# Cross-attention with float32r splits: the output projection in three passes, the heads' chunks split in place, and some low parts moved from GpSimd to VectorE

## The reference, cut to what matters

```python
qh, kh, vh = heads(xn @ Wq), heads(ctx @ Wk), heads(ctx @ Wv)   # 8 heads of 128; 2048 rows each
sim  = qh @ kh.T                                # per head 2048 x 2048
attn = softmax(1.5 * sim * 128 ** -0.5)         # over the keys (the mean shift falls out)
out  = concat(attn @ vh) @ Wout + bout          # Wout: 1024 x 256
x    = x + out
```

## Time and profile before

| | |
|---|---|
| median of 3 runs | 1329.42 us |
| profiled execution, its own time | 1332.3 us |
| span from its first to its last instruction | 1330.2 us |
| busy: PE, DVE, ACT, POOL | 1287.7, 1023.5, 895.9, 907.9 us |
| mean granted clock of TensorE | 0.99 |

### The profile page before, as it was taken

One profiled execution on the slowest core, in us unless ns is written; L12 is line 12 of the kernel. 1 busy time (PEld: TensorE's weight loads), 2 busy tenths in 40 slices (PEclk: granted clock), 3 DMA queues, 4 the chain that ended last, 5 costly groups with the idle time before them and its releaser, 6 DMA issues. The chain is left out here.

```text
span 1330.2 us, 22729 instructions
## 1 busy us (share of the span) xinstructions
PE 1287.7 (97%) x8358; PEld 1077.1 (81%) x8358; DVE 1023.5 (77%) x1628; ACT 895.9 (67%) x1315; POOL 907.9 (68%) x645
## 2 busy tenths in 40 slices
PE   5999999999999999999999999999999999988998
PEld 4688888888887788888888888888888888777998
DVE  6355498759317889999999999999999899985554
ACT  4555433425655878878778778778787777775774
POOL 2544410225410899989989999999999989863553
PEclk9999999999999999999999999999999999997999
DMA  6703032246764989988888888888888888796672
GB/s 219 104 6 74 4 101 81 67 130 245 208 233 140 247 213 231 221 196 216 215 203 215 216 201 218 215 196 221 214 201 217 201 191 208 185 252 244 203 230 76
DMA packets 172377, 241.35 MB, mean 181 GB/s; under 512 B 34179, under 2 KB 78085, under 8 KB 172272
## 3 DMA queue, kind: packets, MB, share of 16 engines
q1 hardware_dynamic: 155040, 208.11, 62.0%
q10 hardware_dynamic: 15184, 25.96, 5.7%
q0 software_dynamic: 2048, 5.90, 1.1%
HBM read 64.79 MB, written 41.32 MB: 80 GB/s over the span
## 5 line engine op out<-in xcount | busy, mean ns | idle before, releaser
L1217 POOL TENSOR_TENSOR xa_pT<-xa_moved,xa_pT 128x1024 fp32r<-128x1024 f32 x246 | 589.0, 2428 | 27.1 <-ACT xa_pT L1735 26.0
L1557 PE MATMUL xa_S<-xa_kT,xa_qT 128*128 128x512 f32 x1536 | 389.1, 401 | 1.2 <-ACT xa_probs L1741 1.2
L1741 ACT ACTIVATE xa_probs<-xa_S,xa_mx_nb_rinv 128x1024 f32<-128x1024 f32 x256 | 285.9, 1117 | 146.8 <-DVE xa_mx_nb_rinv L1339 146.8
L1574 PE MATMUL xa_O<-xa_pT,xa_v 128*128 128x512 f32 x1536 | 377.2, 394 | 2.9 <-DVE xa_pT L1392 2.6
L1336 DVE TENSOR_REDUCE xa_mx_nb_rinv<-xa_S 128x1 f32<-128x1024 f32 x256 | 305.3, 1211 | 78.1 <-PE xa_S L1557 78.0
L1574 PEld LDWEIGHTS xa_O<-xa_pT,xa_v 128*128 128x128 f32 x1536 | 289.0, 189 | 69.9 <-DVE xa_pT L1392 2.9
L1557 PEld LDWEIGHTS xa_S<-xa_kT,xa_qT 128*128 128x128 f32 x1536 | 288.5, 188 | 67.9 <-ACT xa_probs L1741 2.9
L1349 DVE STREAM_TRANSPOSE xa_tq<-xa_probs 128x1024 f32<-128x1024 f32 x256 | 316.7, 1238 | 15.0 <-ACT xa_probs L1741 7.3
L1735 ACT ACTIVATE xa_pT<-xa_moved 128x1024 fp32r<-128x1024 f32 x254 | 253.9, 1050 | 2.1 <-PE xa_O L1574 1.1
L506 PE MATMUL fw_pp<-fw_hT,fw_wqk 128*128 128x512 f32 x384 | 95.0, 405 | 4.3 <-DVE fw_hT L647 4.3
L506 PEld LDWEIGHTS fw_pp<-fw_hT,fw_wqk 128*128 128x128 f32 x384 | 73.4, 194 | 20.7 <-DVE fw_hT L647 3.0
(11 more groups left out here) (247 smaller groups left out, 1679.1 us busy)
## 6 DMA issues: line engine op xcount, KB each, us to landing
xa_moved<-xa_tq SPq DMA_DIRECT2D x508, 256.0 KB, 4.5
heads_k<-ci_outs SPq DMA_DIRECT2D x32, 256.0 KB, 2.0
heads_v<-ci_outs SPq DMA_DIRECT2D x32, 256.0 KB, 2.3
heads_q<-ci_outs SPq DMA_DIRECT2D x32, 256.0 KB, 2.4
xa_chunk<-heads_v ACTq DMA_DIRECT2D x32, 256.0 KB, 4.2
ex_w1s<-in_L_ffn_w_dram SPq DMA_DIRECT2D x8, 1024.0 KB, 7.3
ex_w2s<-in_L_ffn_w_dram SPq DMA_DIRECT2D x8, 1024.0 KB, 9.7
xa_chunk<-heads_q ACTq DMA_DIRECT2D x31, 256.0 KB, 4.2
```

Source lines behind the costliest of these rows:

```text
L1217: pool.tensor_tensor(quadrants(pT[LO], r), unit_moved(r), quadrants(pT[HI], r).bitcast(F32), ALU.subtract).then_inc(lo_ready, 1)
L1557: last = pe.matmul(banks[:, k % 2], qT[a][:, i // GT % 2, q], kT[b][h % 2][:, k * 512:(k + 1) * 512], start=(n == 0), stop=(n == 2))
L1574: last = pe.matmul(O[:], v[a][:, j * P:(j + 1) * P], pT[b][:, r % PRING, k], start=(j == 0 and n == 0), stop=(j == JT - 1 and n == 2))
L1741: act.activation(probs[:, unit % RING], S[:, score_banks(unit)].rearrange("p a b -> p (a b)"), ACT.Exp, bias=nb[:, s % 2:s % 2 + 1], scale ...
```

## The change

1. **Output projection in three passes for groups 0 to 27** (heads 0 to 6, `SPLIT_GROUPS` = 28). ScalarE's `split_high(g)` writes the high part of `oT` (512 columns), and once per head that of `woh` (256 columns). VectorE's `split_low(g)` subtracts for the low parts, that of oT written over oT itself. `out_project` then issues 6 float32r matmuls of 256 columns per half in place of 2 float32 ones, and its first half waits for VectorE's low part. Its slots and those of `add_output` are one later.
2. **Chunks are split in place.** The ring of two is gone. A chunk is loaded into the region of its own low part (`raw_k`, `raw_v`, `raw_q`), and the subtraction writes over it. Its load is issued at the end of the slot before the one in which it is split, and waits for the region's last reader first. The chunks are spread differently over a head's slots.
3. **Low parts of q's chunks on VectorE.** `q_low` is run by VectorE in the slot after ScalarE's high part; only head 0's first q chunk stays with GpSimd.
4. Small ones: head 0's v chunks wait on ScalarE, not GpSimd, for the stores that share their space; the load of `woh` waits for the split of the last one and not for the last projection; the constants of the routing wait for the last split group's projection.

```diff
-        CRING, RING, MRING, PRING = 2, 2, 3, 4
+        RING, MRING, PRING = 2, 3, 4
...
+        raw_k = [home(f"xa_rawk{i}", f"kT{i}", [P, TOK], F32, LO * 4 * TOK) for i in range(2)]
+        raw_v = home("xa_rawv", "v", [P, TOK], F32, LO * 4 * TOK)
+        raw_q = home("xa_rawq", "qT", [P, 2, GCOLS], F32, LO * 4 * 2 * GCOLS)
         woh = sb("xa_wout", [P, D])
-        chunk = home("xa_chunk", "chunk", [P, CRING, UNIT])
+        wohs = [home(f"xa_wouts{a}", "chunk", [P, D], F32R, 4 * (GCOLS + D * a)) for a in (HI, LO)]
...
+        SPLIT_GROUPS = SLOTS // GT - 4
...
-            return SLOTS + OUTPUTS[g, k] if (g, k) in OUTPUTS else (g + 1) * GT + LAG + 2 * k
+            return SLOTS + OUTPUTS[g, k] if (g, k) in OUTPUTS else (g + 1) * GT + LAG + 2 * k + (g < SPLIT_GROUPS)
...
-            plan = {0: ("k", h + 1, 0), 1: ("q", h, 1), 2: ("k", h + 1, 1), 3: ("k", h + 1, 2), 4: ("v", h, 0),
-                    5: ("q", h, 2), 6: ("v", h, 1), 7: ("v", h, 2), 8: ("v", h, 3), 9: ("k", h + 1, 3),
-                    10: ("q", h, 3), 13: ("q", h + 1, 0)}
+            plan = {0: ("k", h + 1, 0), 1: ("q", h, 1), 3: ("k", h + 1, 1), 4: ("q", h, 2), 5: ("v", h, 0), 6: ("v", h, 1),
+                    7: ("v", h, 2), 8: ("v", h, 3), 10: ("q", h, 3), 11: ("k", h + 1, 2), 13: ("q", h + 1, 0),
+                    14: ("k", h + 1, 3)}
...
+        def q_split_at(s):
+
+            return [c for c in chunks_of(s - 1) if c[0] == "q"] if s > 0 else []
+
+        def group_split_at(s):
+
+            g, phase = divmod(s - LAG - GT, GT)
+            return g if phase == 1 and 0 <= g < SPLIT_GROUPS else None
...
@@ vector
+            def q_low(c):
+                dve.wait_ge(chunk_hi, place[c] + 1)
+                dve.tensor_tensor(target(c, LO), staged(place[c]), target(c, HI).bitcast(F32),
+                                  ALU.subtract).then_inc(out_lo, 1)
+
+            def split_low(g):
+                if g % 4 == 0:
+                    dve.wait_ge(out_hi, g + g // 4 + 1)
+                    dve.tensor_tensor(wohs[LO][:], woh[:], wohs[HI][:].bitcast(F32), ALU.subtract).then_inc(out_lo, 1)
+                dve.wait_ge(out_hi, g + g // 4 + 2)
+                dve.tensor_tensor(oTs[LO][:], oT[:], oTs[HI][:].bitcast(F32), ALU.subtract).then_inc(out_lo, 1)
...
                     maxima(s)
+                if s < SLOTS:
+                    for c in q_split_at(s):
+                        q_low(c)
+                    if group_split_at(s) is not None:
+                        split_low(group_split_at(s))
                 if 1 <= s <= SLOTS:
                     transpose(s - 1, 1)
...
@@ tensor, out_project
+                if k == 0 and g < SPLIT_GROUPS:
+                    pe.wait_ge(out_lo, outputs_split(g))
...
+                    if g < SPLIT_GROUPS:
+                        for n, (a, b) in enumerate(PARTS):
+                            last = pe.matmul(output_bank(g, k)[:, m], oTs[a][:, t], wohs[b][:], start=(n == 0), stop=(n == 2))
...
@@ scalar
+            def split_high(g):
+                if g % 4 == 0:
+                    act.wait_ge(wo_in, 16 * (g // 4 + 1))
+                    act.wait_ge(y_mm, 2 * g)
+                    act.activation(wohs[HI][:], woh[:], ACT.Copy).then_inc(out_hi, 1)
+                act.wait_ge(oT_ready, g + 1)
+                act.activation(oTs[HI][:], oT[:], ACT.Copy).then_inc(out_hi, 1)
...
+                if GT <= p and p % GT == 0 and p // GT - 1 < SPLIT_GROUPS:
+                    split_high(p // GT - 1)
                 if s < SLOTS:
                     for c in chunks_of(s):
                         chunk_high(c)
+                    for c in chunks_of(s + 1) if s + 1 < SLOTS else ():
+                        load(place[c])
```

More of the change, by code:

```diff
@@ L904, in cross_block @@
         first_in = [sem(f"xa_first_in{i}") for i in range(FIRST)]
-        chunk_in = [sem(f"xa_chunk_in{i}") for i in range(CRING)]
+        chunk_in = sem("xa_chunk_in")
         chunk_hi, chunk_lo = sem("xa_chunk_hi"), sem("xa_chunk_lo")
@@ L1063, in staged @@
                 return moved[:].rearrange("p r q j n -> p (r q j n)")[:, n * UNIT:(n + 1) * UNIT]
-            return chunk[:, n % CRING]
+            kind, h, part = order[n]
+            cols = slice(part * UNIT, (part + 1) * UNIT)
+            if kind == "k":
+                return raw_k[h % 2][:, cols]
+            return raw_v[:, cols] if kind == "v" else raw_q[:, part % 2]
         def target(c, a):
@@ L1205, in chunk_low @@
                 n = place[c]
[L1206 to L1210, removed]
                 pool.wait_ge(chunk_hi, n + 1)
@@ L1701, in load @@
             def load(n):
[L1702 to L1705, removed]
-                act.dma_start(chunk[:, n % CRING], source(order[n])).then_inc(chunk_in[n % CRING], 16)
-            def chunk_high(c):
-                n = place[c]
-                kind, h, part = c
-                if n < FIRST:
-                    act.wait_ge(first_in[n], 16)
-                else:
-                    act.wait_ge(chunk_in[n % CRING], 16 * ((n - FIRST) // CRING + 1))
+                c = kind, h, part = order[n]
                 if kind == "k" and h >= 2:
@@ L1718, in chunk_high @@
                     act.wait_ge(sim_done, 2 * GT * (4 * h + part - 1))
-                if kind == "v" and h == 0 and part == QUADS - 1:
+                if kind == "v" and h == 0:
                     for u in range(UNITS - OUTS, UNITS):
-                        if u % OUTS == 0:
+                        if u % OUTS == part + 1 or part == QUADS - 1 and u % OUTS == 0:
                             written(act, u)
@@ L1724, in chunk_high @@
                     act.wait_ge(pv_done, 2 * (TILES * h - GT + part) + 2)
+                for u in units_of(c):
+                    written(act, u)
+                act.dma_start(staged(n), source(c)).then_inc(chunk_in, 16)
+            def chunk_high(c):
+                n = place[c]
+                if n < FIRST:
+                    act.wait_ge(first_in[n], 16)
+                else:
+                    act.wait_ge(chunk_in, 16 * (n - FIRST + 1))
                 act.activation(target(c, HI), staged(n), ACT.Copy).then_inc(chunk_hi, 1)
-                if FIRST + CRING <= n + 1 < len(order):
-                    load(n + 1)
             def high_part(r):
@@ L1785, in _ @@
                 copy_out(n)
-            for n in range(FIRST, FIRST + CRING):
-                load(n)
             act.wait_ge(w_lo, 2)
```

52 lines of the change are left out of this document (36 added, 16 removed).

## The result

The kernel after takes 1412.33 us (median of 4 runs, 1408.99 to 1413.80) against 1330.19 us before: a ratio of 1.0614 (95% interval 1.0591 to 1.0636), 82 us slower. The forecast was 1398 us, within 1355 to 1425. Its profiled execution has a span of 1410.5 us against 1330.2, 80.3 us more, and the clock that TensorE was granted is 0.98 in the mean.

The account below looks back on a forecast made before the run. TensorE bound the kernel before; waits for GpSimd would make VectorE the bound, at 105.3 us per head against 95.5. Seven heads at +9.8 give 69 us, so a median of 1398 us, range 1355 to 1425.

Parts of the forecast that it names:

- The bound now, and the slack: Attention slots before the change: TensorE sets the pace at 95.5 us per head; VectorE works 89.3, leaving 6.2 slack.
- The wait as cause: VectorE's new two-SBUF-input instructions wait until GpSimd's running instruction ends, 0.97 us, making VectorE the bound.
- Its size: VectorE's added work per head: seven single instructions at 1.45 us, 10.1, plus the woh and oT pair, 4.1; sum 14.2.
- 0.45 x 4 = 1.8 per head: VectorE's wait for scores queued behind the first projection half, which waits for the low part: 1.8 us per head.
- The sum over VectorE's whole load: VectorE's 89.3 + 14.2 = 103.5 us per head against TensorE's 94.6; with score waits 105.3, +9.8 per head.
- only the last could count, 1.5 us: Head 0's first three q low parts, slots 2, 5 and 11: only slot 11's could cost, 1.5 us.
- Three passes, 0.11 us per half: Projection on TensorE: six float32r matmuls take 0.71 us, each half 0.11 us cheaper, 0.9 us per head.
- Chunks in place at nothing: Chunk loads, issued about one slot (6 us) ahead, land after 4.0 us, 5.5 at most; cost nothing.
- What was to show: Signs: new VectorE instructions 1.2 to 2.0 us, VectorE close to 100%, TensorE about 90%, ScalarE waiting longer for nb, slots 6.6.
- No waiting (1335 and 1323): Rivals without GpSimd waits: late low part stalls TensorE, 1335 us, chance 0.07; or TensorE stays the bound, 1323, chance 0.05.
- Much slower: Rival: VectorE meets each GpSimd instruction at its start, wait 2.41 us, +21.3 per head, 1478 us; chance 0.06 up to that.

Follow-up runs that it names:

- run 2: Kernel after, with VectorE's new low parts written by a one-element reduce_max (copies, subtraction left out): 1332.47 us, ratio 1.0014.
- run 7: Kernel after, with oT's low part subtracted from PSUM a slot earlier, q's and woh's on GpSimd, projection at its old slots: 1330.66 us.
- run 5: Kernel after, plus 20 float32 matmuls of 128 columns on TensorE before the projection's wait in every fourth group: 1401.42 us.
- q_gpsimd: Kernel after, with q's low parts back on GpSimd and the projection split kept: 1408.13 us; four executions took 1386.4 to 1413.9.
- swap: Kernel after, with oT's and woh's low parts moved to GpSimd and q's left on VectorE: 1365.61 us; executions 1358.0 to 1374.1.
- run 6: Kernel after, with q's low parts on GpSimd and oT's and woh's written by one-element maxima, subtraction left out: 1327.02 us.
- run 3: Parts of the change alone; for chunks in place, kernel after with plain float32 projection and q's low parts on GpSimd: 1330.85 us.
- run 9: Kernel after, with GpSimd's low parts of the probabilities in four 512-column instructions per slot instead of two of 1024: 1422.45 us.

## Why the prediction was right, and where it was off

- **The bound now, and the slack.** Right. In the five heads between slots 28 and 108 VectorE was busy 87.2 us per head before and waited 6.4 for the scores (6.2 in the prediction).
- **The wait as cause.** Right. In run 2 the price goes away with the wait, at the same number of instructions in the same places; in run 7 the real subtraction stands on VectorE without waiting, though a slot earlier and without q and `woh` beside it.
- **Its size.** Near, and in part by luck. VectorE's busy time grew from 435.89 to 506.13 us over those five heads, 14.05 per head, where the sum said 14.2:

```profile
584.10:1116.76 532.66, 490.45 (x2161) 393.76 (x2160) 506.13 (x605) 393.51 (x585) 447.10 (x201) 0.98 0.77 189
```

  The single ones take 1.61 us in the mean by their records, which is 1.54 without the overlap of 0.07, instead of 1.45: a wait of 1.06 instead of 0.97 (11.24 us for seven, less 0.55 each). The pair takes 4.5 instead of 4.1 from start to start. That makes 15.2 for the nine, 1.0 more than the sum, and VectorE's other instructions came out 1.2 shorter beside them, partly by more overlap of their records.
- **Waiting for the scores after a projection, "0.45 x 4 = 1.8 per head".** This is the term that was mis-sized. VectorE waits 3.9 us per head for them (19.3 us in 50 waits over the five heads), of which 2.02 + 1.14 stand behind `woh` and oT alone. The prediction worked with scores at full clock, but behind the stall of 4.68 us the clock is down. With the clock held, run 5, the waits are 10.0 us in 50, or 2.0 per head, near the predicted value. So per head 14.05 - 6.4 + 3.9 = 11.55, less 0.7 by which VectorE's other gaps shrank, is the 10.85 measured; 9.8 was predicted. Over seven heads the difference grows by 75.5 us (slots 12 to 124) instead of 69.

```profile
DVE xa_mx_nb_rinv L1373 <- PE xa_S L1613: 19.3, 50, 2.0
```

- **The sum over VectorE's whole load.** The forecast lets every wait count in full once VectorE's slack is spent, wherever it stands. That fits the whole change and fails for its parts, so the near hit on the total is luck to that extent. In the forecast's terms the split of the projection without q is 3 x 1.45 + 4.1 = 8.5 on VectorE, which with the slack of 6.2 and 1.8 for the scores makes +4 us per head; `q_gpsimd` shows 7.86, and VectorE there still waits 5.9 us per head for the scores (29.5 us over the five heads), nearly the 6.4 of before. q alone on VectorE would be 5.8, inside the slack, so next to nothing; `swap` shows 4.98 in the trace of its slowest execution (about 0.8 of it behind oT), and even its fastest is 28 us above before. What the runs show in its place is a price by slot: where the projection waits for the low part (5.2 to 6.7 us with `woh`, 0.65 to 1.8 without) TensorE and VectorE stop in turn, and room in other slots doesn't make up for it, while the four q of the kernel after cost about 2 us per head net by their steps.
- **Head 0, "only the last could count, 1.5 us".** Off: 4.5 us at slot 12, by the q that lost to two GpSimd instructions, and 5.5 in all up to there. 75.5 + 5.5 = 81.0, and the spans differ by 80.3.
- **Three passes, 0.11 us per half.** Right: six matmuls from 709.65 to 710.36 are 0.71 us, plain slots gain 0.05 to 0.12, and run 6 keeps 0.71 us per head of 0.9. **Chunks in place at nothing**: right by run 3. **ScalarE's copies at nothing**: right by runs 2 and 6, which have them and lose nothing.

```profile
709.65 0.40 PE L1650 MATMUL xa_Y<-xa_wouts,xa_oT_hi 128*128 128x256 f32 x2
...
710.36 0.87 PE L1613 MATMUL xa_S<-xa_kT,xa_qT 128*128 128x512 f32 x3
```

- **What was to show.** The instructions at 1.2 to 2.0 us in the mean: q is (1.32), oT is a little above (2.15), those after `woh` are 2.82 (2.9). VectorE close to 100%: it is 95.0 over the five heads. TensorE about 90%: 92% (490.45 of 532.66). ScalarE's idle time per exponential did grow, but more than half of it is now for the transposes (67.9 us from 600 to 1100 us) and not for nb (60.3 us). Slots of 6.6 us: 6.66.
- **The rivals.** No waiting (1335 and 1323): refuted, and runs 2 and 6 (1332.5 and 1327.0 us) show that these times were fair for that case. Much slower, a whole instruction waited each time: not here in the mean, but the q at 466.81 and run 9 show that single ones can wait as long and longer.

## What to carry to other kernels

Before low parts or other work on two SBUF inputs move to VectorE, look at what GpSimd does in that slot: the price isn't only the instruction's 0.6 us but the rest of the GpSimd instruction that is running, too, and a free share of VectorE's time doesn't pay for it where TensorE waits behind it in the same slot. An operand left in PSUM took the wait away here, 653 ns against 2149, at the price of holding the bank. And a stall of TensorE is to be counted with the lower clock after it, which here made 5.2 to 6.7 us out of 3.92.

## What the runs showed that I had not expected

- `tensor_scalar` with one SBUF input waits for GpSimd (1760 and 1066 ns in the mean), a maximum over one element with the same input and output doesn't (676 ns).
- GpSimd waits for VectorE too: 2.85 us instead of 2.40 for the instruction that stands behind one of VectorE's.
- A waiting instruction can lose to more than one GpSimd instruction: two of 2.4 us (5.25 us for 512 columns), and four of 1.22 (5.47 us).
- Dividing GpSimd's work finer made the kernel slower, 1422 against 1412 us, though most single waits got shorter.
